# Narrow attention on one NeuronCore: the maxima of a slot issued on TensorE ahead of its scores and masks

## The reference: what is computed

```python
Q, K, V = heads of (layernorm(x) @ Wq), (ctx @ Wk), (ctx @ Wv)
scores = Q @ K.T * scale + bias        # layer 2: a bias from token positions; layer 3: a mask over keys
m = max(scores, axis=-1)
e = exp(scores - m)
attn = e / (sink + sum(e))             # sink is 1.0 in layer 2, 0.0 in layer 3
x = x + tanh(gate) * (attn @ V) @ Wo
```

## Time and profile before

| | |
|---|---|
| median of 3 runs | 1532.38 us (1531.8 to 1533.9) |
| the profiled execution | 1531.62 us |
| its span on the core | 1529.8 us |
| mean granted TensorE clock | 0.918 |
| PE, DVE, ACT, POOL busy | 88%, 69%, 52%, 44% |
| layer 2 attention with maxima | about 810 to 1056 us of the span |
| layer 3 attention with maxima | about 1240 to 1484 us of the span |

### The profile page before, as it was taken

The page is one execution under the profiler, slowest core; times in us unless marked ns, Lnnn a source line. Parts: engine busy times, 40 slices in busy tenths (PEclk is TensorE's granted clock), DMA queues, the critical chain, the costliest instruction groups (busy, mean ns, idle before and its releaser), DMA issues. The chain is left out here.

```text
span 1529.8 us, 32994 instructions
## 1 busy us (share of the span) xinstructions
PE 1339.7 (88%) x11860; PEld 743.4 (49%) x11868; DVE 1051.6 (69%) x3269; ACT 795.8 (52%) x1144; POOL 678.7 (44%) x542
## 2 busy tenths in 40 slices
PE   6999968748999999999746898999899859999994
PEld 4444454624666666666532333333577624333432
DVE  4988844166766666666478787686466778887876
ACT  2777723245656566565343555556433215655663
POOL 4766613514766676667524243230230073453310
PEclk8999978957999999999966999899799968999997
DMA  4566635446423442230034554330210032242301
GB/s 149 191 227 227 234 129 175 141 143 227 153 82 112 152 159 92 101 139 2 3 83 95 115 101 97 79 79 3 77 27 0 1 70 46 49 76 52 60 6 28
DMA packets 93029, 152.30 MB, mean 100 GB/s; under 512 B 18817, under 2 KB 64028, under 8 KB 89287
## 3 DMA queue, kind: packets, MB, share of 16 engines
q1 hardware_dynamic: 85312, 120.69, 28.0%
q10 hardware_dynamic: 2688, 25.56, 4.3%
q0 software_dynamic: 4880, 4.04, 1.2%
HBM read 93.66 MB, written 45.11 MB: 91 GB/s over the span
## 5 line engine op out<-in xcount | busy, mean ns | idle before, releaser
L1993 DVE CUSTOM_DVE_ANT_0 a_junk<-a_psM,a_madd 128x512 bf16<-128x512 f32 x512 | 331.4, 683 | 74.4 <-issue 69.3
L1936 ACT ACTIVATE a_probs<-a_psE 128x1024 f32<-128x1024 f32 x256 | 261.9, 1023 | 164.0 <-PE a_psE L1813 162.3
L2402 DVE TENSOR_REDUCE a_mx<-a_psM 128x1 f32<-128x512 f32 x236 | 148.2, 669 | 124.5 <-PE a_psM L2226 124.5
L1781 PE MATMUL a_psM<-narrow_k_op,narrow_q_op 57*64 57x512 bf16 (+1 forms) x1024 | 169.1, 423 | 33.6 <-DVE a_mx L1993 21.8
L2363 ACT ACTIVATE a_probs<-a_psE 128x1024 f32<-128x1024 f32 x128 | 130.8, 1024 | 85.9 <-PE a_psE L2248 82.6
L1639 POOL DMA_DIRECT2D narrow_q_op<-a_max_parts x96 | 50.3, 529 | 268.1 <-DVE a_max_parts L2006 268.0
L1825 PE MATMUL a_psO<-a_probs,narrow_values 128*32 128x256 f32 x2048 | 165.6, 398 | 1.8 <-ACT a_probs L1936 1.1
L2196 POOL TENSOR_TENSOR a_half_sum<-a_probs 128x1024 f32<-128x1024 f32 x64 | 150.7, 2355 | 32.8 <-ACT a_probs L2363 32.8
L2244 PE MATMUL a_psE<-a_qT,a_kT 64*128 64x256 f32 x1024 | 134.1, 382 | 0.0
L2260 PE MATMUL a_psO<-a_probs,a_values 128*64 128x256 f32 x1024 | 124.7, 386 | 0.8 <-ACT a_o_raw L2347 0.8
L2384 DVE RECIPROCAL a_o_raw<-a_o_raw 128x256 f32<-128x256 f32 x64 | 111.4, 1741 | 11.0 <-ACT a_o_raw L2347 11.0
(11 more groups left out here) (381 smaller groups left out, 2602.8 us busy)
## 6 DMA issues: line engine op xcount, KB each, us to landing
wide_k<-a_k_stage SPq DMA_DIRECT2D x32, 512.0 KB, 2.6
a_k_part<-wide_k SPq DMA_DIRECT2D x64, 256.0 KB, 3.2
wide_v<-a_v_stage SPq DMA_DIRECT2D x24, 512.0 KB
a_kT<-wide_k ACTq DMA_DIRECT2D x6, 2048.0 KB, 7.9
a_values<-wide_v ACTq DMA_DIRECT2D x6, 2048.0 KB
keys<-a_parts SPq DMA_DIRECT2D x96, 64.0 KB, 2.0
narrow_k_op<-keys SPq DMA_DIRECT2D x30, 192.0 KB
narrow_q_op<-a_y_parts SPq DMA_DIRECT2D x180, 32.0 KB
```

What stands on the lines that cost most here:

```text
L1781: last = pe.matmul(psM[j][c * n:(c + 1) * n, :], q_op[r][group, s // 2, s % 2 * P + c * n:s % 2 * P + (c + 1) * n], k_op[r][group, s // 2, :],
L1936: act.activation(probs[:, head:head + 2, k:k + 2, :], psE[es % 2][:], ACT.Exp).then_inc(exped, 1)
L1993: dve.tensor_tensor_reduce(junk[j][:], psM[j][:], madd[r][:, t, :], 1.0, -3.0e38, ALU.add, ALU.max, mx[r][:, max_place(h, t):max_place(h, ...
L2402: dve.tensor_reduce(mx[r][:, at:at + 1], max_bank(2 * p + t, j, first), AX.X, ALU.max).then_inc(max_read, 1)
```

## The change

The two calls of `maximum` move ahead of `score` and `mask` within a slot. `weigh` and the extra parts stay where they were, and so do all instructions of the other engines.

```diff
                         first = not inner and v == (0 if s >= LAG else 1)
+                        if take_max:
+                            for j in range(2):
+                                maximum(v, r, s, j, not inner and v == 0)
                         if take_exp:
                             if es == 0:
                                 pe.wait_ge(crossed[at], 32 * (w // RING + 1))
                             score(w, at, es, first)
                             mask(at, es)
-                        if take_max:
-                            for j in range(2):
-                                maximum(v, r, s, j, not inner and v == 0)
 
                         quad, t = es // QUAD - 1, es % QUAD
```

## The result

The changed kernel takes 1544.01 us in the median of 9 runs (1541.29 to 1545.6), the kernel before on the same chip 1532.77 (9 runs, 1531.38 to 1540.21). The medians lie 11.2 us apart. The sum had said 10.5 and the time 1542.9.

A forecast was written before the change was run, and what follows sets the result against it. Neither TensorE nor VectorE alone bounds the kernel; lateness of either is paid by both. Layer 3 8.6, layer 2 3.4, clock -1.5 sum to 10.5 us slower, 1542.9 us, range 1537 to 1549 (8 in 10 runs: 1534 to 1552).

The forecast's parts named there:

- The ring: Maxima, scores, masks, weighing per slot: 1.34 us after against 1.35 before, so slots without an extra part gain and cost nothing.
- The lateness of 0.45: Extra parts behind weighing start 0.45 us later after the maxima VectorE is reading; slot 2's normalise pays it whole.
- Slot 8's split: VectorE already waits for slot 8's transpose, so the late split goes on in full: 0.45 us per element.
- Slot 6's add: Add already waits 0.48, but idleness of 0.18 behind it takes up part: 0.27 to 0.29 us per element.
- Slot 0's split: VectorE is the later engine there by 0.35, so 0.10 us is left (bounds 0 and 0.45).
- Layer 2: Layer 2's attention: 3.4 us more without the clock, with 1.1 gained at landed rows in each of elements 1 and 4.
- The term for the clock: Layer 2's two clock falls may go with shorter waits: 0 to 3.2 us gained, half taken, 1.5.
- The rival of the clock: Slot 10's longer stall makes the clock fall in 12 elements: 19 us more, 1562; chance 0.08.
- Faster: VectorE's extra parts have slack, leaving gains at layer 2's landed rows and clock: 10.6 us, 1522; chance 0.08.
- no change: Lateness sinks in TensorE's existing stalls, only the two ends cost, 0.9 and up to 2 us: 1532 to 1535; chance 0.11.
- ScalarE late: Each group's first weighing waits for the exponential as its margin shrinks from 0.3 to 0.1: 11 us more, 1553; chance 0.07.
- this sign of being wrong: The prediction is wrong if exponentials are waited for in slots with maxima; no size given.

The follow-up runs named there:

- only_turn_out_first: Changed kernel with only slot 2's transpose moved right behind the maxima, other extra parts behind weighing; ratio 1.0043 (1.0019 to 1.0067).
- only_splits_first: Changed kernel with only the two transposes of maxima (slots 8 and 0) right behind the maxima; ratio 1.0019 (0.9995 to 1.0042).
- new_order_extras_first: Changed kernel with each slot's extra part right behind the maxima, ahead of scores, masks and weighing; 1534.75 us, ratio 0.9999 (0.9976 to 1.0021).
- vector_parts_later: Changed kernel with VectorE's normalise and add in slots 3 and 7 instead of 2 and 6; ratio 1.0 (0.998 to 1.0021).
- new_order_both_repairs: Changed kernel with VectorE's normalise and add one slot later and the transposes of slots 0 and 8 right behind the maxima; ratio 0.9983 (0.9961 to 1.0006).
- old_order_vector_later: Kernel before with VectorE's normalise and add in slots 3 and 7 instead of 2 and 6; ratio 1.0018 (0.9996 to 1.0039).
- old_order_extras_first_again: Kernel before with each slot's extra part between the maxima and the weighing, second timing; 1530.98 us, ratio 0.9996 (0.9974 to 1.0019).
- layer3_only: Kernel before with the new order in layer 3's attention alone; 1543.35 us against 1536.01, ratio 1.0051 (1.0028 to 1.0074).
- twin_of_before: Kernel before, unchanged, run once more for a second profile; ratio 1.0004 (0.9985 to 1.0023).
- layer2_only: Kernel before with the new order in layer 2's attention alone; 1536.85 us, ratio 1.0006 (0.9982 to 1.0031).

## Why the prediction was right, step by step

The sum of the whole, 10.5 us for a measured 9.5 (7.4 to 11.6), came out right; its terms did so unequally. The table is worked out from VectorE's timeline: the time from the first reading of a slot to the first reading of the next, in element 3 of layer 3, in us. Slots not listed take 13.02 to 13.07 together in every kernel.

| kernel | slots 2 to 5 | 6 and 7 | 8 | 11 | element |
|---|---|---|---|---|---|
| before | 7.62 | 3.81 | 2.43 | 2.44 | 29.33 |
| after | 8.06 | 3.87 | 2.98 | 2.44 | 30.39 |
| only_turn_out_first | 7.50 | 3.88 | 2.98 | 2.44 | 29.87 |
| only_splits_first | 8.06 | 3.89 | 2.31 | 2.43 | 29.73 |
| new_order_extras_first | 7.62 | 3.93 | 2.31 | 2.56 | 29.46 |
| vector_parts_later | 7.92 | 3.62 | 2.58 | 2.44 | 29.58 |
| new_order_both_repairs | 7.91 | 3.63 | 2.32 | 2.43 | 29.33 |
| old_order_vector_later | 7.92 | 3.67 | 2.32 | 2.44 | 29.39 |
| old_order_extras_first_again | 7.38 | 3.81 | 2.32 | 2.44 | 28.98 |

**The ring** (right). Slots without an extra part take the same in both orders, but for slot 7 (below), and the pair that had no row, weighing to maxima, is 0.57 as taken. With it the 7 us either way that the prediction allowed for are settled.

**The lateness of 0.45** (right). The part starts at N + 1.34, and normalise pays 8.06 - 7.62 = 0.44 against 0.45. Taking the move back for that part alone returns 8.06 - 7.50 = 0.56: the 0.44, and 0.12 that the old order lost there.

**Slot 8's split** (right, by way of two rows). The table has 0.55 in slot 8. Slot 7 alone is 0.11 shorter than before (1.24 for 1.35), since VectorE, late from add, finds slot 8's maxima written already. It then waits for slot 8's transpose that much longer: together 0.44 against 0.45. Moving the transposes ahead returns 0.67: the 0.55, and 0.12 (2.43 less 2.31) that the old order lost. My expectation for that kernel had booked the split at 0.18 to 0.35, because I had measured from the start of add to the start of the split, and add's start had itself moved by 0.44. Cost must be read from reading to reading; the start of a waiting part says how late it is, not what it costs. One row under this step was a disturbed one. The stall of 0.38 at slot 10 followed a cast of 0.53 us in the split (916.71), which takes 0.21 in layer 3's elements. The step doesn't hang on it: in element 3 of layer 3 the stretch from slot 9's maxima to slot 10's went from 1.58 (1349.97 to 1351.55) to 2.04 (1357.64 to 1359.68), 0.46 more.

**Slot 6's add** (mis-sized, 0.28 for 0.17). Slot 6 takes 2.63 where it took 2.46. The reading behind add follows it after 0.41 us (1354.31 to 1354.72); I had taken the operation's 0.48 as the least distance. Whether slot 7's 0.11 is booked with the split, as here, or with add is a choice. The single move of the splits measures the split at 0.55 and leaves add with 0.06 to 0.08 (3.87 or 3.89 less 3.81). Either way the two cost 0.61 together, where 0.73 was predicted.

**Slot 0's split** (mis-sized, 0.10 for nothing). Its slot takes 2.32 in both: VectorE reaches the split 0.34 behind the transpose, still from its own readings.

Together 0.44 + 0.44 + 0.17 = 1.05, measured 1.06, predicted 1.28: the element of 30.39 misses the 30.5 to 30.7 that the prediction had named as its sign. For layer 3: six elements 6.4, element 1's split 0.43 (13.26 to 13.69 between its splits), the end 0.43 (13.66 to 14.09): 7.2 where 8.6 was predicted. Measured: 7.4 between the first two profiles' stages (255.9 and 263.3; 263.0 in layer3_only), 7.8 (4.3 to 11.4) by layer3_only's runs. The two other profiles of the old order have 257.6 and 257.8, and 14.13 and 14.16 in element 1's stretch. In both the clock rose some 6 us later, in element 1 instead of the first. The same 6 us, 26 to 32 behind the layer's first reading, in the first profile, in twin_of_before and in the changed kernel (the clock is the third number from the end):

```profile
1276.60:1282.60 6.00, 5.56 (x87) 2.21 (x87) 5.29 (x26) 3.59 (x4) 3.63 (x5) 1.00 0.16 36
1278.80:1284.80 6.00, 6.00 (x67) 2.33 (x65) 4.77 (x21) 2.76 (x3) 3.38 (x5) 0.54 0.10 18
1282.30:1288.30 6.00, 5.29 (x85) 2.14 (x75) 5.29 (x26) 3.88 (x5) 3.49 (x5) 1.00 0.08 18
```

Against all three old profiles the new order's stage is 6.1 us longer. The loss per element is shown in full; the 7.2 for the layer holds between profiles in which the clock rose alike.

**Layer 2** (predicted +1.9; not settled). The mechanism is there: the waits for landed rows went from 7.4 to 1.3, and to 1.2 in layer2_only; the fall of the clock behind the 2.89 wait is gone (1.00 at 950 to 965). But the old order's waits for landed rows are 7.4, 2.9 and 6.2 in three profiles of it, so there was less to save than one profile showed. The mean stage is 264.3 in those three (267.0, 260.0, 266.0) and 266.5 in two of the new order (268.4, 264.6), 2.2 more, within a spread of 7; by its runs the cost is 0.9, from -2.8 to 4.8. Whether the landing gains meet the 1.06 of its elements stays open. The term for the clock, 1.5 less, was half of a range, taken with nothing that told which. Of the two falls that it counts on, the one behind the 2.89 wait went. The other stayed, behind a wait of 1.3 now (0.83 in 865 to 875, as in 860 to 870 before), and a new one came at 1022. That the sum was off by only 1.0 is in part luck: layer 3 was booked 1.2 to 1.5 too high, and nothing shows what layer 2 cost to better than some us.

**The rival of the clock** (not so for the whole). No undisturbed element lost clock, with slot 10's stall at 0.62 + 0.22. Yet one element of layer 2 did, between 1018 and 1028. The timeline of the changed kernel there, for GpSimd, for VectorE and for TensorE:

```profile
1015.42 3.63 POOL L1713 TENSOR_SCALAR a_maddT<-a_maskT 128x1024 bf16<-128x1024 int32 x1
```

```profile
1018.20 0.92 DVE L2004 CAST a_max_parts<-a_max_rest 16x128 bf16<-16x128 f32 x1
```

```profile
1020.11 0.40 PE L1781 MATMUL a_psM<-narrow_k_op,narrow_q_op 57*64 57x512 bf16 x2 [1.32 <-DVE a_mx L1993]
1020.72 0.40 PE L1781 MATMUL a_psM<-narrow_k_op,narrow_q_op 57*64 57x512 bf16 x2 [0.21 <-DVE a_mx L1993]
```

A cast of the split takes 0.92 us instead of 0.22. It lengthens slot 10's stall from 0.62 to 1.32, and the granted clock goes from 2.4 to 1.2 GHz for a while (mean 0.83 of that window). The half element from split to split takes 16.49 where 14.24 is usual: 0.70 from the cast, 1.5 with the clock. It is tempting to say that the longer stall of the new order let this stray cast reach the fall. The rows of twin_of_before, in the old order, speak against a bound that the stall alone sets:

```profile
956.73 0.40 PE L1781 MATMUL a_psM<-narrow_k_op,narrow_q_op 57*64 57x512 bf16 x2 [1.64 <-DVE a_mx L1993]
957.35 0.40 PE L1781 MATMUL a_psM<-narrow_k_op,narrow_q_op 57*64 57x512 bf16 x2 [0.22 <-DVE a_mx L1993]
```

```profile
956.00:966.00 10.00, 8.98 (x130) 4.06 (x130) 7.73 (x37) 4.94 (x8) 4.11 (x4) 1.00 0.25 57
```

Here 1.64 + 0.22 of idleness was followed by no fall, and a wait of 1.99 at 872 in the same profile by none either, while one of 1.30 at 869 in the changed kernel came with a fall. So what decides stays open, and so does whether the new order had a part in the fall. The Trainium skill, "TensorE: Matmul & The Clock Gate", section "A second HAM failure mode: psum-queue depth-cycling", says that short idleness between groups while banks are cycled makes the clock oscillate. The trace agrees at 1.32 + 0.21. It disagrees at 0.62 + 0.22, though the element idles again and again (79.9 us in 149 waits over the layer) and its clock is 1.00, and at 1.64 + 0.22.

**The other rivals.** *Faster* and *no change*: each needed slack on VectorE, and there was none: its idle times of 0.85, 0.92 and 0.57 had been forecast at 0.8 to 0.9, 0.9 and 0.5. *ScalarE late*: in layer 3 the weighings' waits for exponentials are 2.7 us in 5 waits, 2.4 in 4 before. The fifth, 0.31 at 1291.10, is the only one in a slot with maxima, and a weighing's loads idle as long where they wait for nothing (0.31 at 1356.86). Layer 2 has three in its elements 1 and 2, the longest 0.57; before it had none. So this sign of being wrong did show, at a size that costs next to nothing. The rule on weight loads taken ahead, which the prediction cites from the Trainium skill, "TensorE: Matmul & The Clock Gate", section "Architectural detail: the array is 16× 32×32, not 1× 128×128", would have given the no-change time. The measured element is the forecast's, and the loads at 1356.09 and 1356.10 show that none was taken ahead of the one that waits.

## What to carry to other kernels

In a queue that is taken in order, as TensorE's is here, swapping steps inside a loop can leave the loop's own length as it was (1.34 to 1.35 us a slot in both orders); what costs is each thing whose place against another engine's work has moved. List what stands behind the swapped steps, and ask of each how much later it comes after the work that the other engine does ahead of it. Read such a cost from one steady event to the next (here from reading to reading), slot by slot: it repeated to 0.02 us in most profiles, where whole runs of one kernel scattered by 10 to 16.

## What the runs showed of the hardware that was not expected

- The cast of 16 x 128 in the split took 0.21 to 0.28 us mostly, and 0.31 to 0.94 in 31 cases of the fourteen profiles, all in layer 2. All 31 began within one of GpSimd's mask conversions of 3.6 us, and 28 of them ended 0.07 or 0.08 after it did. The Trainium skill, "SBUF — State Buffer", section "SBUF: two separate sides", says that VectorE and GpSimd share a pair of ports, which for some VectorE instructions is a lock: whichever starts first holds the pair to its end, and the other is blocked. The trace agrees in those 28. It does not in the 3 that ended 2.5 us before the conversion did, nor in 44 further casts within such a conversion, which took 0.21 to 0.28.
- From the maxima's second bank to matmuls of the full array 0.33 to 0.34 us, to weighing 0.32, to scores 0.24, all at full clock.
- A stall of 1.64 + 0.22 us and a wait of 1.99 were followed by no fall of the clock, stalls of 1.30 and 1.32 + 0.21 went with one (the rival of the clock, above).
- Identical code of some 815 us ended 11 us apart (812.5 to 823.7) from one execution to another.
